# Cross attention and a top-2 expert layer: stack edges filled by engines, biases as a last column of the weights, fewer waits, other orders

## The chip, the core and the metric

The kernel runs on one core of a Trainium2 chip. The metric is the device time of one execution, in microseconds (us). The core has five engines, each with its own instruction queue: TensorE (PE in the rows, its weight loads PEld), VectorE (DVE), ScalarE (ACT), GpSimd (POOL) and SyncE (SP), which here only issues transfers. Transfers of all queues run on 16 DMA engines. On-chip memory is SBUF, 128 partitions; TensorE writes its products to PSUM, of which there are eight banks of 128 x 512 numbers.

## The reference

Four sequences of 256 tokens with 256 features pass through a cross attention with 16 heads of 16 features, then through a layer of 8 experts of which each token uses 2, each with a gated part of 32 units and a low-rank part of 16.

```
x  = x + attention(layernorm(x), ctx)        # Q, K, V each with a bias; softmax(Q K' / 4) V, then @ Wo.T + bo
h  = layernorm(x)
s  = softmax(h @ G); w = s where it is among the two largest, else 0
gated = silu(h @ gate_w) * (h @ up_w)
x  = x + einsum(gated, w, down_w) + einsum(h @ lora_A, w, lora_B)
```

All is in 32-bit floats.

## The kernel before

Each engine has an order written out by hand, a word for each step: `name:b.i@bank` is step `name` of sequence `b` (0 to 3), part `i`, writing to PSUM bank `bank`; `e:0.0-5` is six steps. `plan` (L88) turns a line of `ORDERS` (L46) into a list, and every engine's block walks through its own list. Between engines, `wait` (L198) waits for the counter of a step's name on the engine that does it. A PSUM bank is written again only when the step that empties it is done (`wait_evacuated`, L201). So the orders alone decide what stands behind what.

The attention, for each sequence b:

- st1 and rs1 compute mean and deviation of x, n1 normalises, xT transposes on TensorE and xTE copies the result out of PSUM. q is the product with Wq, k and v the products of the context with Wk and Wv. Products run as plain 32-bit ones (a record each for two halves, so 4 matmuls are 8 records) or, for k and v of sequences 1 to 3 (`KV_PARTS`), as three products of high and low parts in the type fp32r. chi and clo split the context, wkh/wkl and wvh/wvl the weights.
- Scores use *stacks*: `kstack` and `qstack` hold for each head pair 64 rows a head, four rows of each head feature's place: high, high, low part of k, and a last one; rows 3, 7, ... are the *edge*. The edge of `kstack` is -1, that of `qstack` 0, but in row 63 and 127 it later takes the row maximum (ms), which the product then subtracts. khi, kw, klo and qhi, qw, qlo make the parts; ks0 (two transfers), ks1, qs0 (two) and qs1 carry them into the stacks from SBUF to SBUF. There are `NSTACK` = 3 stacks of each kind; sequence 3 uses those of sequence 0 again. For the first, minus and zeros fill the whole stack on VectorE and GpSimd; for the others fillk and fillq (L301 to L315) transfer the edge from a small tile `edge`, and fillq:3 writes zeros over rows 63 and 127 again.
- max computes scores of a head pair for the row maximum, mx (VectorE, L613) reduces them, mrow transposes the maxima, mrE copies them, attn computes the scores again with the maximum subtracted and the other way round, e takes the exponential (ScalarE, L501). u multiplies by v (tiles of 32 columns), uT and un divide by the sum, o is the output product, x2 adds it and x (to which GpSimd's xo has added the output bias).
- The biases: `biases` is a 128 x 6 array with the columns of bq, bk and bv, loaded by biases; obias loads bo for all 128 partitions. bias (L741) multiplies bv by Wo on TensorE, bp (L593) adds it to bo.

The expert layer: mean and mlow compute column means of its weights `wf`, wfc and wlc subtract them, wfh and wfl split them; st2, rs2 are the second normalisation, x2T the transpose, low the product with the low-rank part and the gate, glu the product with gate_w and up_w, th and h the activation, r1, ex, r2, r3 the weights of the experts, wl and wh the weighting, hT and lT transposes, down the last product, res the last sum, out the store.

TensorE's array has three shapes here: all 128 x 128; for max and attn two tiles of 64 rows that run side by side; for u, and for the 16-column mrow, tiles of 32 columns.

Of the kernel before, what the change touches and what calls it, by code (L numbers as in the profile page):

```python
# [5 lines left out]
F32 = mybir.dt.float32  # L6
# [41 lines left out]
        k:0@0 xT:0@1 bias@2 q:0@1 mean@0 k:1@2 xT:1@3 v:1@4 max:0.0@0 max:0.1@6 q:1@3 max:0.2@4 max:0.3@0 xT:2@2  # L48
        k:2@6 max:0.4@4 max:0.5@2 q:2@7 max:0.6@0 max:0.7@4 v:0@6 max:1.0@0 xT:3@2 max:1.1@4 max:1.2@6 mrow:0@3
        q:3@2 max:1.3@0 max:1.4@4 v:2@3 attn:0.0@6 max:1.5@0 attn:0.1@2 max:1.6@4 attn:0.2@6 max:2.0@0 attn:0.3@2  # L50
        attn:0.4@4 max:1.7@6 max:2.1@0 attn:0.5@2 max:2.2@4 mrow:1@6 u:0.0@7 attn:0.6@0 max:2.3@2 u:0.1@7
        max:2.4@4 attn:0.7@0 k:3@6 max:2.5@2 attn:1.0@4 max:2.6@0 u:0.2@7 attn:1.1@2 attn:1.2@4 u:0.3@7 max:2.7@0
        attn:1.3@2 u:1.0@6 attn:1.4@4 mlow@7 attn:1.5@2 u:1.1@6 mrow:2@0 max:3.0@4 attn:1.6@2 max:3.1@0 o:0@6
        max:3.2@4 attn:2.0@2 max:3.3@0 x2T:0@6 u:1.2@7 attn:1.7@2 max:3.4@0 low:0@6 max:3.5@4 max:3.6@2 u:1.3@7
        attn:2.1@0 glu:0.1@6 attn:2.2@4 max:3.7@0 attn:2.3@2 glu:0.0@7 attn:2.4@4 mrow:3@0 attn:2.5@2 u:2.0@1
        u:2.1@1 attn:2.6@4 attn:2.7@2 o:1@0 u:2.2@1 attn:3.0@4 u:2.3@1 x2T:1@0 attn:3.1@2 attn:3.2@4 v:3@7
        low:1@0 attn:3.3@4 attn:3.4@6 glu:1.0@1 attn:3.5@4 o:2@0 attn:3.6@2 u:3.0@6 u:3.1@6 attn:3.7@4 x2T:2@0
# [12 lines left out]
        uT:0.0 mx:2.5-6 un:0.0 uT:0.1 mx:2.7 un:0.1 uT:1.0 mx:3.0-1 x2:0 wlc mx:3.3 mx:3.2 mx:3.4-6 uT:1.1 mx:3.7  # L70
        un:1.1 un:1.0 st2:0 uT:2.0 un:2.0 x2:1 h:0.0-1 r1:0 uT:2.1 st2:1 un:2.1 r2:0 r3:0 x2:2 r1:1 h:1.0 uT:3.0
        st2:2 un:3.0 r2:1 uT:3.1 un:3.1 h:1.1 r3:1 res:0 r1:2 x2:3 st2:3 r2:2 h:2.0 r3:2 r1:3 h:2.1 r2:3 res:1
        r3:3 wl:3 h:3.1 h:3.0 wh:3 res:2 res:3
# [818 lines left out]
```

## Time and profile before

| | us |
|---|---|
| median of 3 runs | 125.38 (125.12 to 125.75) |
| the profiled execution | 126.23 |
| its span, first to last instruction | 124.4 |
| TensorE busy | 112.7 (91%) |
| VectorE busy | 91.1 (73%) |
| ScalarE busy | 66.9 (54%) |
| GpSimd busy | 47.3 (38%) |

The profile is of one execution, the times are of others. A matmul's end is modelled, so a busy TensorE need not be at its peak. In the chain of waits each piece is what the next one waited for, or the work before it on the same engine. A time in a timeline is counted from the first instruction; `[2.43 <-PE ...]` behind a row is idle time of that engine in front of it, and what ended it.

### The profile page before, as it was taken

The numbers are of one execution on the slowest core, as the hardware profiler recorded it, in microseconds if no ns is written. First come the engines' busy times: TensorE is split into PE (matmuls) and PEld (weight loads), VectorE is DVE, ScalarE is ACT, GpSimd is POOL, SyncE is SP. The second block draws the span as 40 slices with busy tenths as digits, with TensorE's granted clock in tenths as the row PEclk, the third lists the DMA queues.
The fourth block names the chain that finished last, engine by engine and source line by source line (L and its number), as shares of the span: only waits on it lengthen the run. The fifth ranks groups of instructions, "written<-read, shape, count | busy, mean of one in ns | idle before, by whom it ended". The sixth has DMA issues, their size and how long they took to land.

```text
span 124.4 us, 2498 instructions
## 1 busy us (share of the span) xinstructions
PE 112.7 (91%) x884; PEld 83.4 (67%) x884; DVE 91.1 (73%) x191; ACT 66.9 (54%) x113; POOL 47.3 (38%) x78
## 2 busy tenths in 40 slices
PE   6970699999999879999999999999999999999790
PEld 6840476978778655856667666578666788866570
DVE  5553274298999999799899797799288688796601
ACT  0570302777866895598655387788957204314300
POOL 7881873076996950040004003025603444240000
PEclk9999558999999999999999999999999999999999
DMA  3979992994294000183000000000000002002022
GB/s 85 344 205 389 386 368 96 310 305 178 84 365 146 3 8 5 65 312 142 5 0 5 0 0 11 0 0 0 5 0 0 0 5 84 0 3 84 0 84 84
DMA packets 9845, 12.96 MB, mean 104 GB/s; under 512 B 922, under 2 KB 6378, under 8 KB 9834
## 3 DMA queue, kind: packets, MB, share of 16 engines
q1 hardware_dynamic: 8458, 11.23, 25.8%
q10 hardware_dynamic: 1376, 1.58, 3.7%
q8 instruction: 7, 0.11, 0.3%
q14 instruction: 4, 0.03, 0.1%
HBM read 4.34 MB, written 1.05 MB: 43 GB/s over the span
## 4 chain that ended last, share of the span: by engine, by line
PE 81%; DMA 8%; ACT 5%; SPq 2%; issue 1%; DVE 1%
PE unit L689 29%; PE unit L798 13%; DMA wo<-woT 8%; PE unit L788 7%; PE unit L772 7%; PE unit L807 6%; ACT probs L501 4%; PE unit L853 3%; PE unit L855 3%; PE unit L854 3%; PE unit L814 2%; PE unit L745 2%; PE unit L752 2%; PE unit L840 1%; PE unit L733 1%; PE unit L778 1%
## 5 line engine op out<-in xcount | busy, mean ns | idle before, releaser
L613 DVE TENSOR_REDUCE rowmax<-unit 128x4 f32<-128x1024 f32 x32 | 37.6, 1220 | 6.0 <-PE unit L772 6.0
L501 ACT ACTIVATE probs<-unit 128x1024 f32<-128x1024 f32 x32 | 31.6, 1030 | 10.3 <-PE unit L788 10.1
L798 PE MATMUL unit<-probs,vaug 128*32 128x256 f32 x256 | 16.5, 384 | 0.0
L788 PE MATMUL unit<-qstack,kstack 64*128 64x256 f32 x128 | 14.3, 310 | 0.5 <-ACT probs L501 0.2
L772 PE MATMUL unit<-kstack,qstack 64*128 64x256 f32 x128 | 13.5, 305 | 0.6 <-DVE rowmax L613 0.3
L788 PEld LDWEIGHTS unit<-qstack,kstack 64*128 64x128 f32 x128 | 9.5, 185 | 6.7 <-issue 4.6
L772 PEld LDWEIGHTS unit<-kstack,qstack 64*128 64x128 f32 x128 | 9.3, 185 | 4.4 <-issue 2.6
L798 PEld LDWEIGHTS unit<-probs,vaug 128*32 128x32 f32 x256 | 7.0, 109 | 5.6 <-issue 1.1
L554 DVE BATCH_NORM_STATS2 stats<-xs 128x6 f32<-128x256 f32 x16 | 5.9, 409 | 6.3 <-DMA xs<-x 6.3
L438 POOL TENSOR_TENSOR x2T_lo<-x2T,x2T_hi 128x512 fp32r<-128x512 f32 x3 | 3.8, 1283 | 16.9 <-ACT x2T L516 16.9
L412 POOL TENSOR_TENSOR k_lo<-k_whole,k_hi 128x512 fp32r<-128x512 f32 x3 | 3.8, 1278 | 15.1 <-ACT k_whole L482 15.1
L689 PE MATMUL unit<-xT,wq 128*128 128x256 f32 x32 | 9.5, 450 | 0.0
L689 PE MATMUL unit<-wf,x2T 128*128 128x136 f32 (+1 forms) x40 | 8.3, 347 | 0.0
L689 PEld LDWEIGHTS unit<-xT,wq 128*128 128x128 f32 x32 | 7.0, 226 | 1.5
L807 PE MATMUL unit<-wo,attnT 128*128 128x256 f32 x32 | 7.9, 389 | 0.0
L617 DVE STREAM_TRANSPOSE uT<-unit 128x512 f32<-128x512 f32 x8 | 5.7, 708 | 2.3 <-PE unit L798 2.3
L482 ACT ACTIVATE q_hi<-unit,bias_sb 128x256 fp32r<-128x256 f32 x8 | 3.4, 471 | 6.7 <-PE unit L689 6.7
L430 POOL TENSOR_SCALAR vare<-mv 128x2 f32<-128x2 f32 x4 | 0.9, 234 | 14.9 <-DVE mv L557 14.9
L745 PE MATMUL unit<-wo,bias_sb 128*128 128x256 f32 x4 | 2.1, 674 | 4.9 <-DMA wo<-woT 4.9
L807 PEld LDWEIGHTS unit<-wo,attnT 128*128 128x128 f32 x32 | 5.8, 190 | 1.1
L689 PEld LDWEIGHTS unit<-wf,x2T 128*128 128x128 f32 x40 | 5.4, 190 | 1.6 <-issue 1.4
L679 DVE TENSOR_TENSOR xs<-unit,xs 128x512 f32<-128x512 f32 x4 | 2.8, 688 | 4.0 <-PE unit L855 4.0
(123 smaller groups left out, 224.7 us busy)
## 6 DMA issues: line engine op xcount, KB each, us to landing
kstack<-k_hi SPq DMA_DIRECT2D x8, 256.0 KB, 3.9
qstack<-q_hi SPq DMA_DIRECT2D x8, 256.0 KB, 2.4
xs<-x SPq DMA_DIRECT2D x4, 256.0 KB, 9.5
kstack<-k_lo SPq DMA_DIRECT2D x4, 256.0 KB, 3.1
qstack<-q_lo SPq DMA_DIRECT2D x4, 256.0 KB, 2.5
out<-xs SPq DMA_DIRECT2D x4, 256.0 KB, 2.1
wf<-wffn ACTq DMA_DIRECT2D x1, 648.0 KB, 11.2
cT<-ctxT ACTq DMA_DIRECT2D x2, 256.0 KB, 6.4
```

The costliest lines, as they stand in the source:

```text
L412: pool.tensor_tensor(lo[:, b % 2], whole[:], hi[:, b % 2].bitcast(F32), ALU.subtract).then_inc(done[name], 1)
L438: pool.tensor_tensor(x2T_lo[:], x2T[:, b % 2], x2T_hi[:].bitcast(F32), ALU.subtract).then_inc(done["x2lo"], 1)
L501: act.activation(probs[:, n % NPAIR], unit[BANK["attn", b, i] // 2][:], ACT.Exp, scale=SCALE)\
L554: ins = dve.bn_stats(stats[:, w, b, t], src[:, t])
L613: dve.tensor_reduce(rowmax[:, b % 2, :, :, i].rearrange("p t j -> p j t"), unit[BANK["max", b, i] // 2][:], AX.X, ALU.max).then_inc(done[" ...
L617: dve.transpose(uT[:, i].rearrange("p h n c -> p (h n c)"), work[BANK["u", b, 2 * i]].rearrange("p h s -> p (h s)")).then_inc(done["uT"], 1)
L689: ins = pe.matmul(dst, left(i, k), right(j, k), start=(n == 0), stop=(n == len(steps) - 1))
L745: ins = pe.matmul(dst[:, 0], bv_sb[:, k:k + 1].to_broadcast([P, P]), wo[:, k], start=(k == 0), stop=(k == KT - 1))
L772: ins = pe.matmul(pair[:, j, t], qstack[b][rows, i, t * P:(t + 1) * P], kstack[b][rows, i], start=True, stop=True)
L788: ins = pe.matmul(pair[:, j, t], kstack[b][rows, i, t * P:(t + 1) * P], qstack[b][rows, i], start=True, stop=True)
L798: ins = pe.matmul(dst[QUAD * j:QUAD * (j + 1), i % 2], vaug[:, b % NVALUE, t, 4 * i + j], probs[:, n % NPAIR, j % 2, t], start=(t == 0), s ...
L807: ins = pe.matmul(dst[:, t], attnT[:, b % 2, k, t * P:(t + 1) * P], wo[:, k], start=(k == 0), stop=(k == KT - 1))
```

## The change

1. *Edges.* The steps minus, zeros, fillk and fillq go. In their place kfill and qfill fill a whole stack, for b below 3: kfill:2 and kfill:0 on VectorE, qfill:0 and qfill:2 on GpSimd, qfill:1 and kfill:1 on ScalarE, as a copy of a column of `edge`, which shrinks to 128 x 2. Every transfer into a stack waits for its fill. Row 63 and 127 are left out of the max product, which so has 63 rows for each tile, and need no zeros.
2. *Biases.* bk, bq and bv become a 257th column of Wk, Wq and Wo, so rows of 1028 bytes are loaded; bo is loaded as one row, and bias adds it with a third product, of one row of ones and that row. bp only copies.
3. *Waits.* `wait` notes for each pair of engines the furthest step waited for, and leaves out a wait for an earlier one.
4. *Orders.* All five are written anew.

```diff
     "scalar": """
-        c:0 wq biases obias c:1 wf wkh wvh khi:0 xTE:0 n1:1 qhi:0 khi:1 xTE:1 kw:1 vE:1 n1:2 qhi:1 qw:1 xTE:2
...
+        c:0 wq c:1 bo qfill:1 kfill:1 wkh wvh khi:0 xTE:0 vE:0 n1:1 qhi:0 xTE:1 n1:2 khi:1 kw:1 qhi:1 qw:1 n1:3
...
+        known = {}
+
         def wait(engine, name, b=0, i=0):
-            engine.wait_ge(raised[ON[name, b, i]][name], TURN[name, b, i])
+            stage = name, b, i
+            if known.get((engine, ON[stage]), -1) < PLACE[stage]:
+                known[engine, ON[stage]] = PLACE[stage]
+                engine.wait_ge(raised[ON[stage]][name], TURN[stage])
+
+        def wait_in(engine, loaded, count=16):
+            if (engine, loaded.name) not in known:
+                known[engine, loaded.name] = count
+                engine.wait_ge(loaded, count)
...
             if name == "wk":
-                engine.dma_start(wk[:], view[:, :, 0:D]).then_inc(wk_in, 16)
+                engine.dma_start(wk[:], view[:, :, 0:D + 1]).then_inc(wk_in, 16)
...
-            if name == "biases":
-                engine.dma_start(bias_sb[:], biases).then_inc(bias_in, 16)
-            if name == "obias":
-                engine.dma_start(bo_sb[:], bo.partition_broadcast(P)).then_inc(out_bias_in, 16)
+            if name == "bo":
+                engine.dma_start(bo_row[:], bo).then_inc(bo_in, 16)
...
-                if name == "fillk":
-                    wait(sp, "edge")
-                    sp.dma_start(kstack[b][3:P:4].bitcast(F32),
-                                 edge[:, 0].bitcast(F32).unsqueeze(1).to_broadcast([QUAD, PAIRS, T])).then_inc(k_stacked[b], 16)
...
                 if name == "ks1":
-                    if b == 0:
-                        wait(sp, "minus")
+                    if b < NSTACK:
+                        wait(sp, "kfill", b)
...
+                if name in ("kfill", "qfill"):
+                    act.wait_ge(raised["vector"]["edge"], 1)
+                    dst, n = (kstack[b], 0) if name == "kfill" else (qstack[b], 1)
+                    act.copy(dst[:].rearrange("p i t -> p (i t)"), edge[:, n:n + 1].to_broadcast([P, PAIRS * T]))\
+                        .then_inc(done[name], 1)
...
                     for o in range(KT):
-                        ins = act.activation(dst[:, o], work[BANK[of, b, 0]][:, o], ACT.Identity, bias=bias[:, o:o + 1])
+                        ins = act.activation(dst[:, o], work[BANK[of, b, 0]][:, o], ACT.Identity, bias=bias[:, o, D:])
...
+                if name == "kfill":
+                    dve.memset(kstack[b][:].bitcast(F32), -1.0).then_inc(done["kfill"], 1)
...
                     for k in range(KT):
-                        ins = pe.matmul(dst[:, 0], bv_sb[:, k:k + 1].to_broadcast([P, P]), wo[:, k],
-                                        start=(k == 0), stop=(k == KT - 1))
-                    ins.then_inc(done["bias"], 1)
+                        pe.matmul(dst[:, 0], wo[:, k, D:].to_broadcast([P, P]), wo[:, k, 0:D], start=(k == 0), stop=False)
+                    pe.matmul(dst[:, 0], warm[0:1], bo_row[:], start=False, stop=True).then_inc(done["bias"], 1)
...
                         for j in range(2):
-                            rows = slice(HALF * j, HALF * (j + 1))
+                            rows = slice(HALF * j, HALF * (j + 1) - 1)
```

The issue queue of SyncE from its start, before. `wk`, `wv`, `wo` and `cT` are weights and context, `xs` is x; names in brackets are what a row waits for.

```order
L252 DMA xs<-x 128x2x256
L257 DMA wk<-wattn 128x2x256
L261 DMA wv<-wattn 128x2x256
L252 DMA xs<-x 128x2x256
L308 DMA qstack<-edge 32x8x256 [waits edge_by_vector]
L269 DMA wo<-woT 128x512
L252 DMA xs<-x 128x2x256
L308 DMA qstack<-edge 32x8x256 [waits edge_by_vector]
L252 DMA xs<-x 128x2x256
L254 DMA cT<-ctxT 128x2x256
L303 DMA kstack<-edge 32x8x256 [waits edge_by_vector]
L323 DMA kstack<-k_hi 32x4x512 [waits khi_by_scalar,minus_by_vector]
```

The same queue in the changed kernel:

```order
L264 DMA xs<-x 128x2x256
L269 DMA wk<-wattn 128x2x257
L273 DMA wv<-wattn 128x2x256
L264 DMA xs<-x 128x2x256 x2
L277 DMA wf<-wffn 128x2x648
L266 DMA cT<-ctxT 128x2x256
L279 DMA wo<-woT 128x514
L325 DMA kstack<-k_lo 32x4x512 [waits kfill_by_vector]
L264 DMA xs<-x 128x2x256
L318 DMA kstack<-k_hi 32x4x512 [waits khi_by_scalar]
```

`wf` has come over from ScalarE's queue; the last load of x (x:2) stands behind the transfer of k_lo and its wait for kfill:0, which stands behind klo:0 on VectorE.

ScalarE from its start, before:

```order
L254 DMA cT<-ctxT 128x2x256
L259 DMA wq<-wattn 128x2x256
L263 DMA bias_sb<-biases 128x6
L265 DMA bo_sb<-bo 128x256
L254 DMA cT<-ctxT 128x2x256
L267 DMA wf<-wffn 128x2x648
L453 ACT_TABLE_LOAD
L453 CAST wk_hi<-wk 128x512 [waits wk_in]
L453 CAST wv_hi<-wv 128x512 [waits wv_in]
L482 ACTIVATE k_hi<-unit,bias_sb 128x256 [waits bias_in,k_by_tensor]
```

and in the changed kernel:

```order
L266 DMA cT<-ctxT 128x2x256
L271 DMA wq<-wattn 128x2x257
L266 DMA cT<-ctxT 128x2x256
L275 DMA bo_row<-bo 1x256
L450 ACT_TABLE_LOAD
L450 CAST qstack<-edge 128x2048 [waits edge_by_vector]
L450 CAST kstack<-edge 128x2048 [waits edge_by_vector]
L455 CAST wk_hi<-wk 128x512 [waits wk_in]
L455 CAST wv_hi<-wv 128x512 [waits wv_in]
L483 ACTIVATE k_hi<-unit,wk 128x256 [waits wk_in,k_by_tensor]
```

Two issues are gone, and two fills of whole stacks stand between the table load and the first cast.

TensorE at its start, before (`warm` is a run without use, `unit` is PSUM; the rows are k:0, xT:0, bias, q:0, mean):

```order
L694 MATMUL unit<-warm 128x128 x10
L689 MATMUL unit<-cT,wk 128x256 x4
L733 MATMUL unit<-ident,xn 128x128 x4
L745 MATMUL unit<-wo,bias_sb 128x256 x2
L689 MATMUL unit<-xT,wq 128x256 x4
L752 MATMUL unit<-wf,mean 128x512 x2
```

and in the changed kernel:

```order
L697 MATMUL unit<-warm 128x128 x10
L692 MATMUL unit<-cT,wk 128x256 x4
L736 MATMUL unit<-ident,xn 128x128 x4
L692 MATMUL unit<-wv,cT 128x256 x4
L692 MATMUL unit<-xT,wq 128x256 x4
L761 MATMUL unit<-wf,mean 128x136 x2
L754 MATMUL unit<-wf,mean 128x512 x2
L748 MATMUL unit<-wo 128x256 x2
L749 MATMUL unit<-bo_row,warm 128x256
```

The product that needs `wo` has moved from in front of q:0 to behind mean, and v:0 and mlow have come forward.

TensorE behind the last row maximum, before: attn:2.4, mrow:3, attn:2.5, u:2.0 and 2.1, attn:2.6 and 2.7, o:1, u:2.2, attn:3.0, u:2.3, x2T:1.

```order
L788 MATMUL unit<-qstack,kstack 128x256 x4
L778 MATMUL unit<-ident,rowmax 16x128 x2
L788 MATMUL unit<-qstack,kstack 128x256 x4
L798 MATMUL unit<-probs,vaug 32x256 x16
L788 MATMUL unit<-qstack,kstack 128x256 x8
L807 MATMUL unit<-wo,attnT 128x256 x4
L798 MATMUL unit<-probs,vaug 32x256 x8
L788 MATMUL unit<-qstack,kstack 128x256 x4
L798 MATMUL unit<-probs,vaug 32x256 x8
L814 MATMUL unit<-ident,xs 128x128 x4
```

and in the changed kernel, from mrow:3 on:

```order
L780 MATMUL unit<-ident,rowmax 16x128 x2
L790 MATMUL unit<-qstack,kstack 128x256 x12
L800 MATMUL unit<-probs,vaug 32x256 x24
L790 MATMUL unit<-qstack,kstack 128x256 x4
L809 MATMUL unit<-wo,attnT 128x256 x4
L790 MATMUL unit<-qstack,kstack 128x256 x12
L800 MATMUL unit<-probs,vaug 32x256 x8
```

Steps of one shape have been put together: three attn steps in a row, three `u` steps in a row. From the last row maximum to the last `u` of sequence 3 the shape changes 23 times before and 15 times now.

## Rows read from the trace of the kernel before

**Rows 1.** The page: the span in 40 slices of 3.11 us, tenths busy.

```profile
PE   6970699999999879999999999999999999999790
...
PEclk9999558999999999999999999999999999999999
DMA  3979992994294000183000000000000002002022
GB/s 85 344 205 389 386 368 96 310 305 178 84 365 146 3 8 5 65 312 142 5 0 5 0 0 11 0 0 0 5 0 0 0 5 84 0 3 84 0 84 84
```

**Rows 2.** The chain of waits: start us, us, what; head, and one later piece.

```profile
3.58 10.06 DMA wo<-woT
...
13.68 2.07 PE unit L745 x4
15.76 3.41 PE unit L689 x8
19.17 1.93 PE unit L752 x4
...
41.50 4.60 ACT probs L501 x5
```

**Rows 3.** Windows: length, busy us (instructions) by engine, clock, DMA share, GB/s.

```profile
24.30:72.90 48.60, 47.55 (x454) 34.36 (x454) 43.91 (x46) 35.00 (x57) 19.89 (x22) 1.00 0.30 107
72.90:121.20 48.30, 47.32 (x357) 34.50 (x355) 35.26 (x118) 24.27 (x43) 13.10 (x26) 1.00 0.05 18
```

**Rows 4.** The chain of waits: pieces behind another shape and behind their own.

```profile
30.31 1.92 PE unit L689 x8
...
48.72 1.00 PE unit L798 x16
49.72 0.43 PE unit L772 x4
50.16 0.24 PE unit L788 x4
...
57.69 0.66 PE unit L759 x4
...
74.65 1.86 PE unit L798 x32
...
100.91 1.73 PE unit L807 x8
```

**Rows 5.** Timeline of VectorE: start us, us, line, operation, idle time before it.

```profile
27.44 2.36 DVE L613 TENSOR_REDUCE rowmax<-unit 128x4 f32<-128x1024 f32 x2 [0.23 <-PE unit L772]
```

**Rows 6.** Timeline of all engines: instructions of the head, and a longer cast.

```profile
1.96 1.76 DVE L567 MEMSET kstack<- 128x2048 f32 x1 [0.38 <-issue]
...
3.85 1.28 ACT L453 ACT_TABLE_LOAD   x1 [3.85 <-issue]
...
4.22 0.48 SPq L252 DMA_DIRECT2D xs<-x  x1
...
5.82 0.62 ACT L453 CAST wk_hi<-wk 128x512 fp32r<-128x512 f32 x1 [0.68 <-DMA wk<-wattn]
...
8.77 0.59 ACT L469 COPY xT<-unit 128x512 f32<-128x512 f32 x1
...
14.93 0.75 DVE L554 BATCH_NORM_STATS2 stats<-xs 128x6 f32<-128x256 f32 x2 [3.19 <-DMA xs<-x]
...
21.14 1.29 DVE L600 TENSOR_TENSOR wf<-wf,unit 128x512 f32<-128x512 f32 x2 [0.18 <-PE unit L752]
24.85 2.36 DVE L613 TENSOR_REDUCE rowmax<-unit 128x4 f32<-128x1024 f32 x2 [2.43 <-PE unit L772]
...
36.37 1.05 ACT L456 CAST wf_hi<-wf 128x1024 fp32r<-128x1024 f32 x1
```

**Rows 7.** DMA issues: line, engine, count, KB each, median us from issue to landing.

```profile
kstack<-k_lo SPq DMA_DIRECT2D x4, 256.0 KB, 3.1
qstack<-q_lo SPq DMA_DIRECT2D x4, 256.0 KB, 2.5
```

More of the change, by code:

```diff
@@ L47 @@
     "tensor": """
[L48 to L57, printed above, removed]
@@ L58 @@
-        hT:0@1 lT:0@6 glu:1.1@7 u:3.2@1 u:3.3@1 low:2@0 down:0@6 o:3@7 glu:2.0@6 lT:1@0 hT:1@1 x2T:3@7 glu:2.1@0
-        low:3@1 down:1@2 lT:2@3 glu:3.1@4 hT:2@5 glu:3.0@0 lT:3@1 down:2@2 hT:3@0 down:3@0
+        k:0@0 xT:0@1 v:0@2 q:0@1 mlow@0 mean@2 bias@3 xT:1@4 k:1@5 max:0.0@0 max:0.1@6 q:1@3 max:0.2@0 max:0.3@4
+        max:0.4@6 v:1@2 max:0.5@0 xT:2@3 k:2@6 max:0.6@0 max:0.7@2 q:2@7 max:1.0@4 max:1.1@0 mrow:0@6 k:3@2
+        max:1.2@4 max:1.3@6 v:2@3 max:1.4@0 attn:0.0@4 max:1.5@6 attn:0.1@2 attn:0.2@4 max:1.6@0 max:2.0@2 xT:3@6
@@ L67 @@
+        wfh xTE:2 vE:1 khi:2 kw:2 qhi:2 mrE:0 qw:2 khi:3 kw:3 vE:2 e:0.0-2 xTE:3 e:0.3-4 e:0.6 mrE:1 e:0.5 qhi:3
+        e:0.7 qw:3 e:1.0-3 vE:3 e:1.4-5 mrE:2 e:1.6 x2hi:0 e:1.7 x2w:0 e:2.0 lowE:0 e:2.1-4 mrE:3 th:0.1 e:2.5
+        ex:0 e:2.6-7 e:3.0-3 th:0.0 e:3.4-6 x2hi:1 lTE:0 x2w:1 e:3.7 lowE:1 hTE:0 th:1.0 ex:1 x2hi:2 x2w:2 th:1.1
+        lowE:2 ex:2 x2w:3 lTE:1 th:2.1 th:2.0 lowE:3 hTE:1 th:3.1 ex:3 hTE:2 lTE:2 th:3.0 lTE:3 hTE:3
     """,
     "vector": """
-        warm edge minus st1:0 n1:0 st1:1 st1:2 klo:0 bp st1:3 qlo:0 wfc mx:0.0-7 mx:1.0-6 mx:2.0 mx:1.7 mx:2.1-4
@@ L70 @@
[L70 to L73, printed above, removed]
+        warm edge kfill:2 st1:0 n1:0 st1:1 klo:0 kfill:0 wlc qlo:0 st1:2 st1:3 bp wfc mx:0.0-2 mx:0.4-5 mx:0.3
@@ L77 @@
-        xo:1 xo:3 qlo:2 clo:3 xo:2 qlo:3 wfl xo:0 klo:3 x2lo:0 rs2:0 x2lo:1 rs2:1 wl:0 wh:0 rs2:2 x2lo:2 wl:1
-        wh:1 rs2:3 wl:2 wh:2
+        ident earlier qfill:0 ones rs1:0 wkl rs1:1 wvl chi:1 clo:1 rs1:2 rs1:3 chi:2 clo:2 qlo:1 klo:1 chi:3
+        clo:3 qfill:2 klo:2 qlo:2 xo:3 xo:0 klo:3 xo:1 xo:2 wfl qlo:3 x2lo:0 rs2:0 wl:0 wh:0 x2lo:1 rs2:1 rs2:2
+        x2lo:2 wl:1 rs2:3 wh:1 wl:2 wh:2
     """,
     "sync": """
-        x:0 wk wv x:1 fillq:2 wo x:2 fillq:1 x:3 c:2 fillk:1 ks0:0 wd ks1:0 qs0:0 qs1:0 c:3 fillk:2 ks0:1 ks1:1
@@ L82 @@
-        qs0:1 qs1:1 qs0:2 ks1:2 ks0:2 ms:0 qs1:2 ms:1 fillq:3 qs0:3 qs1:3 ks0:3 ks1:3 ms:2 ms:3 out:0 out:1 out:2
-        out:3
+        x:0 wk wv x:1 x:3 wf c:3 wo ks1:0 x:2 ks0:0 qs0:0 qs1:0 c:2 wd ks0:1 qs0:1 qs1:1 ks1:1 ks0:2 ms:0 qs0:2
+        ks1:2 qs1:2 ms:1 ks1:3 qs0:3 ks0:3 qs1:3 ms:2 ms:3 out:0 out:1 out:2 out:3
     """,
@@ L583, in _ @@
                     of = name[0]
-                    hi, lo, bias = (k_hi, k_lo, bk_sb) if of == "k" else (q_hi, q_lo, bq_sb)
+                    hi, lo, bias = (k_hi, k_lo, wk) if of == "k" else (q_hi, q_lo, wq)
                     if b >= 2:
@@ L593, in _ @@
                 if name == "bp":
[L594 to L596 removed]
+                    dve.wait_ge(raised["tensor"]["bias"], 1)
+                    dve.tensor_copy(bo_sb[:], work[BANK["bias", 0, 0]][:, 0]).then_inc(done["bp"], 1)
                 if name == "wfc":
[L598 removed]
+                    dve.wait_ge(raised["tensor"]["mean"], 1)
                     for k in range(KT):
@@ L603, in _ @@
                 if name == "wlc":
-                    wait(dve, "mlow")
+                    dve.wait_ge(raised["tensor"]["mlow"], 1)
                     for k in range(KT):
@@ L762, in _ @@
                     if i == 0:
-                        if b == 0:
-                            wait(pe, "minus")
-                            wait(pe, "zeros")
+                        if b < NSTACK:
+                            wait(pe, "kfill", b)
+                            wait(pe, "qfill", b)
                         wait_stacked(pe, "k", b)
```

134 lines of the change are left out of this document (65 added, 69 removed).

## The prediction, made before the changed kernel had run

> **What bounds the kernel now.** Read the slices first [rows 1]: from slice 7 on TensorE is busy nine or ten tenths almost to the end, at full clock. The first 21 us are another matter: an idle stretch in slices 3 and 4, and half the clock (1.2 of 2.4 GHz) in slices 4 and 5, after that idleness. The chain of waits [rows 2] says what the head is: 10.06 us for the transfer of `wo`, for which bias waits in front of q:0; then bias, q:0 and mean, 2.07, 3.41 and 1.93. A product of q's size at full clock takes 1.73 [rows 4], so q:0 alone lost 1.7 us to the clock. From the first maximum at 24.4 to 121.1 the chain is nearly all TensorE; the one other large piece is 4.60 us of exponentials, where the two kinds of score step alternate [rows 2].
>
> Next, who else is near the bound. I cut the rest where the last row maximum ends [rows 3]. From 24.3 to 72.9 TensorE is busy 47.55 us and VectorE 43.91 of 48.6; the maxima come in pairs of 2.36 with gaps of 0.23 [rows 5]. Both are full, and a gain of one alone is worth little. From 72.9 to 121.2 TensorE is busy 47.3 of 48.3 and VectorE 35.3: there TensorE alone sets the time.
>
> **What a change of tile shape costs** [rows 4]. A score step (four matmuls on 64-row tiles) takes 0.43 behind another shape, 0.24 behind its own: 0.19. A full-array product of 8 records takes 1.92 behind scores and 1.73 behind its own shape: 0.19. Two `u` steps take 1.86, one takes 1.00: 0.14. I take 0.19 on average. The row transposes mrow use 16 columns and count with `u`.
>
> **The head, step by step.** Gone are biases, obias and four 256 KB fills from `edge`, with a 16 KB one; `wf` moves to SyncE's queue ahead of `wo`, and x:2 moves behind the first stack transfer.
> - *Transfers.* Of what is gone, fillq:2, biases and obias share the queues with `wo` and `wf` now. Slice 2 shows the DMA engines 90% busy or more at 205 GB/s, against 389 and 386 in slices 4 and 5 [rows 1]; the 24-byte rows of biases and the broadcast of `bo` are what is peculiar to it. In the change, `wf` and all that may go with it (x:0, wk, wv, x:1, x:3; c:0, wq, c:1) are 2.8 MB. 85 and 344 GB/s over two slices of 3.11 us are 1.3 MB by 6.2 us; the rest at 385 takes 3.8, and with about one for the end of a transfer `wf` lands near 11, `wo` near 12.3, against 14.5 and 13.6 now.
> - *ScalarE.* Four issues instead of six end at 2.8, then the table load of 1.28 [rows 6]. The fills qfill:1 and kfill:1 have no row. Casts of 512 and 1024 columns take 0.62 and 1.05, so 2048 should take 1.05 + 2 x 0.43 = 1.91 each; below that stands VectorE's fill of the same tile, 1.76, above it four casts of 512, 2.48 [rows 6]. I take the casts' slope, the same kind of instruction. So 4.1 + 3.8 = 7.9; wkh and wvh to 9.2, khi:0 (0.84, two activations) to 10.0, xTE:0 (0.59 [rows 6]) to 10.6, vE:0 and n1:1 (0.6 and 1.1) to 12.3, qhi:0 to 13.2. The fills lie on the path of q:0: without them it could start 1.8 us earlier.
> - *TensorE.* xT:0 ends at 8.7 as now; v:0, pulled forward, fills until 10.5 (1.72), so there is no pause and I expect the full clock. q:0 from 10.6 to 12.3; mlow 0.46 (its piece of 0.66 less a change [rows 4]); mean 1.72; bias 0.86, and its third product, of one row of `bo`, 0.43 and two changes: 16.2. xT:1 0.44 and k:1 1.4: 18.0. No row shows a product with one row; between 0.43 and 1.1, it isn't last here.
> - *Stacks and the first maximum.* VectorE: klo:0 to 10.9, kfill:0 (1.76) to 12.7. Only then does SyncE issue ks1:0, and x:2, ks0:0, qs0:0, qs1:0 are queued behind that wait. Issues take 0.55 to 0.6 each, so qs1:0 goes out at 16.2 and lands 2.5 later, 18.7 [rows 7]. x:2, issued at 13.4, has no row on an idle queue. By q_lo's 2.5 and k_lo's 3.1 [rows 7] it lands near 16.4; by its own time now, issued 4.22 and read 14.93 [rows 6], it takes 10.7 and lands at 24. I take 3.0, as only `wo` and c:3 are ahead of it and nearly done. VectorE then does st1:2 and st1:3 (1.0 each), bp (0.4) and wfc (1.29 [rows 6]): **first maximum at 20.1**, against 24.85 now [rows 6], a gain of **4.75**. Bounds: 19.2 if x:2 isn't last (the stacks are), 23 if TensorE falls to the low clock.
>
> By the Trainium skill, DMA: Bandwidth & Descriptors, How a descriptor splits into AXI transactions, a row that does not begin on a 256-byte boundary costs beats for bytes that are thrown away; this speaks against the extra column, which makes rows of 1028 bytes at an odd pitch. Estimated from that page, the four loads concerned would take about a fifth longer, some 0.5 us in the head; no row here shows such a load.
>
> **From the first to the last maximum.** TensorE has 42 changes of shape in this stretch, before and after. glu:0.1, mlow and v:0 leave it (1.39 + 0.46 + 1.72), two attn steps, v:1 and v:3 enter (0.47 + 2.83): 0.27 less. VectorE has wlc out (0.5) and st2:0 in (1.0). Both engines are full, so 48 us stay 48: **0**. The bounds: -2.7, if the waits under the 4.60 us of exponentials go, to +2.1, two exponentials more for ScalarE that nothing hides.
>
> **Behind the last maximum.** 15 changes of shape instead of 23: 8 x 0.19 = 1.5. glu:0.1 comes in, v:3 and two attn steps are out: 1.42 + 0.47 - 1.39 = 0.5. TensorE sets the time alone here, so **2.0** arrives, unless ScalarE gets in front: from the last maximum to the last attn TensorE has 14.6 us of steps, and ScalarE 11 exponentials of 1.03 with some 3 us beside them.
>
> **Edits with one answer.** The built program keeps the 64-row tile for maxima of 63 rows, so their price stays. Of the waits left out I make nothing: the steps of 0.24 carry waits now and show no gap. A bias read from the weights' last column changes no instruction's size. fillq:3, 16 KB, was hidden.
>
> **Sum.** The profiled execution took 126.23, with a span of 124.4; it lies 0.85 above the median of 125.38. 4.75 + 0 + 2.0 = 6.75 makes it 119.5, and the median **118.6**.
>
> **Rivals.**
> *The middle gains too.* From 40.9 to 46.2 eleven score steps of 0.24, 2.6 us, take 5.3. The new order mixes xT:3 and other steps in. If that returns 2.0, and x:2 isn't last (0.7), the time is 115.9. For it: the gaps of [rows 5] end with TensorE. Against it: VectorE has 44 us to do in those 48.
> *The low clock stays.* If `wf` lands at 14 or later, TensorE idles behind q:0 as it does now behind xT:0; mean and bias, xT:1 and k:1 then run at [rows 2]'s prices, 3 us more: 121.6. Against it: the transfers left out ahead of `wf`.
> *The second half waits.* If the 8 changes are no saving, or ScalarE is late by as much, 2.0 stays away: 120.6. For it: a long row of full-array work now stands at the end, with little between the exponentials.
> *Slower.* Everything on VectorE up to the first maximum, and n1:2 with khi:1 behind it on ScalarE, is now queued behind x:2, which is issued behind the waits for klo:0 and kfill:0. If x:2 takes its present 10.7 instead of 3.0, the first maximum is at 27.8, TensorE stands idle for 8 us and comes back at the low clock, 1 us at least: 118.6 + 7.7 + 1.0 = 127.3. It decides from a landing 9 us after the issue. Against it: at 13.4 hardly a load is ahead.
>
> **Chances.** Forecast (117 to 120) 0.50; middle gains 0.17; low clock 0.12; second half waits 0.15; slower 0.04; in all, a time within 0.5% of now 0.02 (about what a measurement of this kernel can tell from no change). The range of 8 in 10 takes in the rivals on the fast side: 115.6 to 121.6. Faster 0.94, same 0.02, slower 0.04.
>
> **What would show it.** Right: no wait for `wo` in the chain; a granted clock of 1.00 from 6 to 21; two instructions near 1.9 on ScalarE at 4 to 8; first rowmax near 20; the last one ends 47 to 49 later; 46 from there to the last product. Wrong: q:0 later than 11.5, a clock under 1 behind 9, more than 49 between first and last maximum, or TensorE waiting over 1 us in all for ScalarE behind it.

## The result, and the profile after

The changed kernel takes 120.03 us (median of 4 runs, 119.24 to 121.01), the kernel before 125.32 in the same rounds: a ratio of 0.960, with a 95% interval of 0.9545 to 0.9656. The profiled execution took 120.67, with a span of 118.9. The four took 120.67, 119.24, 119.38 and 121.01 us, at mean clocks of 1.0, 1.0, 1.0 and 0.986. A ratio here and below leaves out the executions that are more than 1.5% above the fastest of their kernel, while medians and ranges are those of all.

The page of the changed kernel, the slices that answer to [rows 1], of 2.97 us each (all slices are counted from 0):

```profile
PE   6989997799998799989999999999999999999780
...
PEclk9999999999999999999999999999999999999999
DMA  2998079845627000580000000000000000202022
GB/s 77 361 367 301 0 269 342 284 176 218 258 81 281 8 0 1 206 313 23 0 11 0 0 1 10 0 0 0 6 0 0 0 0 0 88 8 88 0 88 88
```

The idle stretch and the half clock of slices 3 to 5 are gone, and slice 2 moves 367 GB/s where it moved 205. What is left of the head's idleness is in slices 6 and 7.

The chain of waits of the changed kernel, its head, which answers to [rows 2] (start us, us, what):

```profile
1.28 4.95 DMA wk<-wattn
...
6.27 3.79 PE unit L692 x8
...
10.09 0.85 ACT k_hi L483 x2
...
12.21 1.78 DVE kstack L568
14.01 0.65 SPq L325
...
17.87 3.58 DMA qstack<-q_lo
```

No piece waits for `wo` any more. In its place stands the filling of the first stack: k:0 (L692), khi:0, klo:0, the fill kfill:0 on VectorE (L568), then six issues of SyncE in a row, and behind them qs1:0 with its landing of 3.58. The timeline of the changed kernel shows the rows of this stretch, against [rows 6]:

```profile
4.26 1.90 ACT L450 CAST qstack<-edge 128x2048 fp32r<-128x2048 f32 x1
...
6.06 1.89 ACT L450 CAST kstack<-edge 128x2048 fp32r<-128x2048 f32 x1
...
17.27 0.69 PE L749 MATMUL unit<-bo_row,warm 1*128 1x256 f32 x2
...
17.70 0.75 DVE L555 BATCH_NORM_STATS2 stats<-xs 128x6 f32<-128x256 f32 x2 [1.62 <-DMA xs<-x]
...
21.59 0.74 PE L774 MATMUL unit<-kstack,qstack 63*128 63x256 f32 x8 [1.64 <-DMA qstack<-q_lo]
...
22.14 2.36 DVE L616 TENSOR_REDUCE rowmax<-unit 128x4 f32<-128x1024 f32 x2 [0.99 <-PE unit L774]
```

Windows of the changed kernel, columns as in [rows 3], cut where the last maximum ends:

```profile
22.10:69.10 47.00, 45.60 (x460) 33.80 (x457) 43.91 (x48) 35.45 (x58) 23.38 (x24) 1.00 0.29 109
69.10:115.70 46.60, 45.61 (x346) 33.88 (x344) 34.97 (x114) 22.76 (x41) 12.38 (x23) 1.00 0.06 18
```

So the profiled executions differ in three places: first maximum at 22.14 instead of 24.85, 2.71 us; from it to the end of the last one 46.99 instead of 48.06, 1.07; from there to the last product 46.48 instead of 48.20, 1.72. Together 5.50 of the 5.56 between 126.23 and 120.67.

### The profile page after: what moved, and what is told of

It reads as the page before. It is cut to its first block, busy times and chain, and to the rows that moved or that the text cites. A ratio compares the mean times of both kernels' runs of the same rounds, so it can differ in the third digit from the quotient of the medians.

```text
span 118.9 us, 2315 instructions
## 1 busy us (share of the span) xinstructions
PE 110.0 (93%) x886; PEld 83.1 (70%) x886; DVE 91.5 (77%) x192; ACT 70.4 (59%) x115; POOL 49.4 (42%) x79
## 4 chain that ended last, share of the span: by engine, by line
PE 62%; DVE 12%; DMA 10%; SPq 5%; issue 3%; ACT 2%; POOL 1%; POOLq 1%; DVEq 0%; ACTq 0%
PE unit L692 19%; PE unit L800 12%; PE unit L790 8%; PE unit L774 7%; DMA qstack<-q_lo 6%; PE unit L809 5%; DMA wk<-wattn 4%; PE unit L855 2%; PE unit L857 2%; PE unit L856 2%; DVE rowmax L616 2%; SPq L333 2%; DVE kstack L568 1%; PE unit L816 1%; SPq L325 1%
## 5 line engine op out<-in xcount | busy, mean ns | idle before, releaser
L774 PE MATMUL unit<-kstack,qstack 63*128 63x256 f32 x128 | 12.7, 302 | 2.3 <-DMA qstack<-q_lo 2.3
L790 PE MATMUL unit<-qstack,kstack 64*128 64x256 f32 x128 | 13.2, 304 | 0.8 <-ACT probs L502 0.5
L774 PEld LDWEIGHTS unit<-kstack,qstack 63*128 63x128 f32 x128 | 9.1, 186 | 5.7 <-issue 4.0
L289 POOL TENSOR_TENSOR low<-low,weight_low 128x128 f32<-128x128 f32 x6 | 2.3, 403 | 14.5 <-DVE weight_hid L668 14.5
L692 PE MATMUL unit<-wf,x2T 128*128 128x136 f32 (+1 forms) x40 | 8.2, 344 | 0.0
L692 PE MATMUL unit<-xT,wq 128*128 128x256 f32 x32 | 7.8, 386 | 0.0
L409 POOL TENSOR_TENSOR q_lo<-q_whole,q_hi 128x512 fp32r<-128x512 f32 x3 | 3.9, 1284 | 7.5 <-ACT q_whole L483 7.5
L532 ACT ACTIVATE hid<-unit,half_rstd 128x256 f32<-128x256 f32 x8 | 3.8, 474 | 5.1 <-PE unit L692 5.1
L692 PEld LDWEIGHTS unit<-wf,x2T 128*128 128x128 f32 x40 | 5.7, 190 | 1.3 <-issue 1.0
L692 PEld LDWEIGHTS unit<-xT,wq 128*128 128x128 f32 x32 | 5.8, 190 | 0.9
L697 PE MATMUL unit<-warm 128*128 128x128 f32 x20 | 4.6, 430 | 1.1 <-DVE warm L566 1.1
```

Of the source, the lines that this page charges most:

```text
L409: pool.tensor_tensor(lo[:, b % 2], whole[:], hi[:, b % 2].bitcast(F32), ALU.subtract).then_inc(done[name], 1)
L692: ins = pe.matmul(dst, left(i, k), right(j, k), start=(n == 0), stop=(n == len(steps) - 1))
L697: pe.matmul(unit[3][:, 1, 0, 0:P], warm[:], warm[:], start=True, stop=True)
L774: ins = pe.matmul(pair[:, j, t], qstack[b][rows, i, t * P:(t + 1) * P], kstack[b][rows, i], start=True, stop=True)
L790: ins = pe.matmul(pair[:, j, t], kstack[b][rows, i, t * P:(t + 1) * P], qstack[b][rows, i], start=True, stop=True)
```

## The experiments

Three groups of kernels ran, each with the kernel before beside it, which took 125.68 us (e1 to e4), 125.70 (e5 to e8) and 125.26 (e9 to e12) in the median; so 0.4 us between two groups says little. Each experiment is told by three marks of its profiled execution: start of the first maximum, length from there to the end of the last, length from there to the last product. The kernel before has 24.85, 48.06 and 48.20, the changed one 22.14, 46.99 and 46.48.

### Orders alone: is it the place of bias?

In the kernel before, bias goes behind mean, and bp behind wfc:

```diff
-        k:0@0 xT:0@1 bias@2 q:0@1 mean@0 k:1@2 xT:1@3 v:1@4 ...
+        k:0@0 xT:0@1 q:0@1 mean@0 bias@2 k:1@2 xT:1@3 v:1@4 ...
```

> The kernel before with one step moved: TensorE does bias behind mean instead of in front of q:0 (and VectorE does bp behind wfc). All transfers, fills, waits and the rest of the orders stay. Theory A (the head was lost because bias waits for wo in front of q:0, an order, not the transfers): q:0 starts near 9.5 us instead of 15.8 and costs 1.9 instead of 3.4; then wf, which landed at 14.5, is last, mean and bias follow it, and the first row maximum comes 2 to 3 us earlier: 122.5 to 123.5. Theory B (what counts is the transfers that the fills and biases put in front of wo and wf): mean still waits for wf, the clock still falls in that wait, and the time stays within 1 us of 125.3.

Measured: 127.34 us (126.52 to 127.9), ratio 1.0121 (1.0077 to 1.0166): 1.2% slower, with the first maximum at 25.96 instead of 24.85. Neither theory had that. Its timeline:

```profile
9.85 1.97 PE L689 MATMUL unit<-xT,wq 128*128 128x256 f32 x8 [1.06 <-ACT xT L469]
...
16.32 3.78 PE L752 MATMUL unit<-wf,mean 128*128 128x512 f32 x4 [4.51 <-DVE k_lo L589]
```

q:0 runs as soon as xT:0 is there, 5.7 us earlier. But mean then waits 4.5 us. It writes the PSUM bank of k:0, which klo:0 has to empty first, and on VectorE klo:0 stood behind st1:2 and the landing of x:2 (read at 14.47). Mean itself runs at half speed, 3.78 for [rows 2]'s 1.93. The wait moved on to the next late transfer, so the place of bias alone was not the head's cost. That the late transfers were is what the next run shows.

### The change with the old orders

Edges, biases and waits as in the change, the five orders as before, as far as they can be.

> The changed kernel's code (fills by engines, bias columns, fewer waits, 63-row maxima) with the orders of the kernel before; the removed steps are taken out and the fills put in at near places (kfill:0 and kfill:2 early on VectorE, qfill:0 and qfill:2 on GpSimd, qfill:1 and kfill:1 behind the loads on ScalarE). Theory A (the orders carry the gain: bias moved, steps of one shape put together): only the shorter head of transfers is left. wo lands near 10 instead of 13.6, so 2 to 3 us come back in the head and nothing behind it: 122.5 to 123.5. Theory B (code and transfers carry it): 120 to 121. The end behind the last row maximum should stay at 48 us by A.

Measured: 120.97 us (120.36 to 121.67), ratio 0.9606 (0.9544 to 0.9667), the same as the change. Marks: 19.51, 47.93, 48.00. Windows and the head's wait:

```profile
19.51:67.44 47.93, 47.01 (x449) 33.65 (x446) 43.91 (x46) 34.40 (x56) 21.40 (x23) 1.00 0.27 101
67.44:115.44 48.00, 47.30 (x357) 34.49 (x355) 35.61 (x116) 24.24 (x43) 13.09 (x26) 1.00 0.05 18
```

```profile
10.35 1.13 PE L749 MATMUL unit<-wo 128*128 128x256 f32 x4 [1.60 <-DMA wo<-woT]
```

This splits the change. Edges, biases and waits bring 5.34 us of head and little elsewhere (48.06 to 47.93, 48.20 to 48.00), though bias still stands in front of q:0: `wo` lands 7.5 us after its issue instead of 10.06. The new orders bring 0.94 in the middle and 1.52 behind, and lose 2.63 in the head. About 1 us of that loss belongs to the profiled execution of the change alone, in which k:0 ran slowly: where it ran fast, the first maximum is at 20.98 (e3) and 21.11 (e10), a loss of 1.5 to 1.6. In the medians the orders bring nothing. At a mean clock of 1.0 they may bring 1 us: 120.36 and 120.50 here, 119.24, 119.38 and 120.67 in the change.

### All waits made

```diff
-            if known.get((engine, ON[stage]), -1) < PLACE[stage]:
+            if True:
...
-            if (engine, loaded.name) not in known:
+            if True:
```

> The changed kernel with every wait made again, also those for steps that an earlier wait already covers; nothing else changes. My prediction put the left-out waits at zero: 119.2 to 120.8, as the changed kernel. The rival: TensorE pays for a wait that is already met. It has about 100 of them more; at 20 ns each behind the first maximum that would be 1.5 to 2 us: 121.5 to 122.

Measured: 120.7 us (119.81 to 121.55), ratio 0.9559 (0.9479 to 0.9639). Its two runs at a mean clock of 1.0 took 119.81 and 119.94, those of the change 119.24, 119.38 and 120.67, so in the times the waits stay inside the spread. The trace shows more. From the end of the last maximum to the last product e3 takes 46.8 us, and the change and the seven other kernels that have its orders in this stretch (e4, e6, e7, e8, e10, e11, e12) all take 46.5. Up to the end of glu:1.0, 21.0 us behind the last maximum, e3 and the change are alike, so TensorE's own row pays nothing there. The loss comes later, where the work goes through VectorE and GpSimd, and part of it is a wait of TensorE for GpSimd that the change does not have; first the change, then e3:

```profile
103.78 0.65 PE L842 MATMUL unit<-ident,hid 128*128 128x128 f32 x4
```

```profile
104.58 0.63 PE L842 MATMUL unit<-ident,hid 128*128 128x128 f32 x4 [0.26 <-POOL hid L298]
```

So leaving waits out brings 0.3 us behind the last maximum, by one trace of e3 against eight, and perhaps 0.5 in all.

### The fill of the first stack taken off the path

```diff
-        warm edge kfill:2 st1:0 n1:0 st1:1 klo:0 kfill:0 wlc qlo:0 ...
+        warm edge kfill:0 st1:0 n1:0 kfill:2 st1:1 klo:0 wlc qlo:0 ...
```

First together with twelve warm-up products instead of ten (e4), then the fill alone (e7), then the warm-up alone (e10).

> The changed kernel with two changes in the head: kfill:0 goes to the front of VectorE (kfill:2 takes its place behind n1:0), so that ks1:0 waits for klo:0 only and SyncE's row behind it starts 2.0 us earlier; and 12 useless products instead of 10 in front of k:0, which close the pause of 0.5 us before it, after which k:0 ran at half speed (3.78 instead of 1.99). Theory A (both lie on the path to the first row maximum: k:0 - khi:0 - klo:0 - kfill:0 - ks1:0 ... qs1:0): first maximum at 18.5 to 19.5 instead of 22.1, time 117 to 118, and the runs lie closer together than 119.2 to 121.0. Theory B (the landing of the stacks or x:2 takes up what the fill gives): first maximum at 21 or later, 119 to 120.

> The changed kernel with kfill:0 at the front of VectorE alone, with the 10 useless products. It parts the run that had both edits. If the fill carries the gain, first maximum near 20 and 118 to 118.5 in the runs in which k:0 runs at full speed, and 1.8 us more in those in which it doesn't; if the pause in front of k:0 carries it, 119 to 120.

> The changed kernel with twelve warm-up products instead of ten, and nothing else. It asks whether the idle time in front of k:0 is what makes k:0 run at half speed (3.8 us instead of 2.0) in some runs. Theory A (the pause matters): k:0 near 2.0 in every run, runs close together at 119.2 to 119.5. Theory B (the pause does not matter): runs spread from 119.2 to 121, median near 120.0 as for the changed kernel.

Measured: e4 117.75 us (117.58 to 117.83), ratio 0.9347 (0.9308 to 0.9385), marks 19.28, 46.90, 46.49; e7 117.79 (117.74 to 117.84), ratio 0.9384 (0.933 to 0.944), marks 19.25, 46.94, 46.48; e10 120.95 (119.44 to 122.05), ratio 0.962 (0.9551 to 0.969), first maximum 21.11. The fill alone brings all of it: 2.2 us in the median. The warm-up brings nothing, and its theory A fell: k:0 took 2.12 us in the profiled execution, and the time was 120.95 all the same. Nor does the pause in front of k:0 decide its speed. In the change k:0 waited 0.54 us and took 3.79. In e3, whose head is the same, it waited 0.74 and took 1.99, and in e5, told below, it waited longer still:

```profile
5.92 1.99 PE L693 MATMUL unit<-cT,wk 128*128 128x256 f32 x8 [0.98 <-DMA wk<-wattn]
```

What made it slow in the change stays open.

The chain of e10 is the forecast's own path, and shows each of its steps at its size:

```profile
4.28 1.90 ACT qstack L450
6.17 1.32 ACT kstack L450
...
9.78 0.88 DVE k_lo L593 x2
10.66 0.38 issue
11.03 1.77 DVE kstack L568
...
16.67 3.57 DMA qstack<-q_lo
```

Two rows of e10's timeline show what follows the wait, then one of e7's, with the fill off the path:

```profile
20.37 1.13 PE L774 MATMUL unit<-kstack,qstack 63*128 63x256 f32 x8 [2.31 <-DMA qstack<-q_lo]
...
21.43 3.20 PE L692 MATMUL unit<-xT,wq 128*128 128x256 f32 x8
```

```profile
18.71 0.74 PE L774 MATMUL unit<-kstack,qstack 63*128 63x256 f32 x8 [0.74 <-DMA qstack<-q_lo]
```

After 2.3 us of idleness the score step and q:1 ran slowly, at a granted clock of 0.72 from 18 to 24 us. e10's four runs took 119.44, 120.95, 120.96 and 122.05 us at mean clocks of 1.0, 0.986, 0.986 and 0.966; where TensorE waits 0.74 us (e7), four runs lie within 0.1 us. So the fill on the path costs twice: its own time, and in some runs the clock. In the traces of e10 and e7 that is 1.86 us up to the first maximum, and another 1.35 from there to the end of the last (48.29 against 46.94).

### The fills as transfers again

The kernel with the old orders (e2), with the edges of stacks 1 and 2 carried by four transfers of 256 KB as before, and no fill on ScalarE; the biases stay a column.

> As the run with the old orders, but the edges of stacks 1 and 2 are filled by transfers again (fillk and fillq, 4 x 256 KB, at their old places), and the two casts on ScalarE and the fills kfill:2 and qfill:2 are gone; the biases stay columns of the weights. It parts the changed code into its two halves. Theory A (the fills in front of wo and wf were most of the head: fillq:2 is 256 KB ahead of wo, and biases only 3 KB): wo lands at 12 to 13, first maximum at 22.5 to 23.5, time 123.5 to 124.5. Theory B (the loads of biases with their 24-byte rows were it): wo lands near 10.5 and ScalarE is 3.8 us free, first maximum at 19 to 20, 120 to 121 as with the fills on engines.

Measured: 125.11 us in the median of ten runs between 122.27 and 126.55, at mean clocks from 0.998 down to 0.954; the ratio, 0.9809 (0.9747 to 0.9871), rests on the three fastest. The profiled execution, 126.43, is one of the longest, so its marks (25.39, 47.94, 48.04) overstate the head. Its timeline:

```profile
11.74 2.07 PE L749 MATMUL unit<-wo 128*128 128x256 f32 x4 [1.69 <-DMA wo<-woT]
...
14.89 3.78 PE L693 MATMUL unit<-xT,wq 128*128 128x256 f32 x8
```

The half clock is back, as in the kernel before. Since the time goes with the clock, compare runs of one clock. At 0.983 to 0.986 the kernel before takes 124.3 to 125.2 us, e5 123.2 and 123.3, e2 121.4 and 121.7. So the four transfers cost some 1.7 us net of the work that the engines' fills put in their place, and what e5 shares with the change (biases, `bo`, waits) brings 1 to 2. The rest of what the transfers cost is the clock: seven of e5's ten runs were at 0.972 or lower, none of e2's four. With the clock, e5 stands 4.1 us above e2 in the median, and the kernel before 4.7. The landings show the transfers at work. The first two transfers of k_hi land 6.7, 7.0 and 7.3 us after their issue in the kernel before, e1 and e5, and 3.0 to 3.2 in the change and e2.

### Single transfers, each by itself

A load of 128 rows of 24 bytes, as biases was, added to e4 at its old place, into a tile that nothing reads (e6); the broadcast of `bo`, 128 KB, added to the kernel e8 of the next heading at its old place (e11); four transfers of the kind of fillk and fillq, 1 MB, added to e8 (e12).

> The fastest kernel so far (fill 0 first, 12 useless products) with one transfer more: 128 rows of 24 bytes into an unused tile, behind wq in ScalarE's queue, where biases was loaded before; nothing uses it, the last engine only waits for it at the end. It prices the small rows alone. Theory A (small rows take engine time out of all proportion): a slice near 200 GB/s comes back, wf lands 1.2 to 1.6 us later than at 7.3 after its issue, TensorE waits for it behind q:0, and the time rises by 0.5 to 1.5 to 118.3 to 119.3. Theory B (128 packets are nothing; the broadcast and the fills were the slow part): wf lands within 0.4 us, 117.8.

> The kernel of e8 with one more load, of 128 KB: bo for all 128 partitions, issued by ScalarE where before issued it, into a tile that nothing reads. Theory A (it shares the queues with what is loaded at the time and slows it by its share): wf and wo land 0.3 to 0.4 us later than in e8, the time stays within 0.3 of 116.84. Theory B (the broadcast is what held slice 2 of the kernel before at 205 GB/s): wf lands 1 us later or more, and mean behind it, 117.3 or more.

> The kernel of e8 with four more transfers of 256 KB each on SyncE's queue, of the kind of fillk and fillq (32 rows of 1 KB, each repeated eight times), behind x:1, x:3, c:3 and the third of them. They write into the tile of the exponentials before it is used; the stacks are filled by the engines as in e8. Theory A (these transfers were the cost of the head of the kernel before): 1 MB at some 380 GB/s puts wf back by 1.4 us and wo and x:2 by 2.8, the clock falls in some runs, 118.5 to 121. Theory B (the queues have room while ScalarE fills): within 0.5 of 116.84.

Measured: e6 117.7 us (117.68 to 117.82), nothing against e4's 117.75, and `wf` lands 7.4 us after its issue instead of 7.3: theory B. e11 117.98 (117.91 to 118.25), ratio 0.9428 (0.9394 to 0.9461), against e8's 116.84: 1.1 us. e12 119.62 (119.5 to 119.69), ratio 0.9553 (0.9527 to 0.958): 2.8 us. The rate in the slices of e11's page:

```profile
GB/s 62 359 222 389 385 367 255 161 278 140 147 277 92 6 0 45 371 139 0 6 6 0 0 11 0 0 0 0 6 0 0 0 0 0 90 8 90 0 90 90
```

The broadcast makes slice 2 fall from e8's 354 to 222 GB/s, near the 205 of [rows 1]. In e5, which has the fills' transfers but not the broadcast, slice 2 is at 373. So the slow slice is the doing of one 128 KB load. `wf` lands 8.8 us after its issue instead of 7.4, `wo` 9.1 instead of 7.7, as theory B said. But mean did not wait for `wf`, so the 1.1 us did not come the way I had written. The chain of e11 shows it:

```profile
3.63 1.28 ACT L453
...
12.45 3.88 DMA xs<-x
16.35 0.76 DVE stats L558 x2
```

ScalarE starts its table load at 3.63 instead of 2.95, since it issues one load more and the one for `bo` takes 0.77 instead of 0.57, and this puts x:2's issue back from 11.77 to 12.45. Then x:2 is read 3.88 after its issue instead of 3.20, and is now last in the head: first maximum at 19.73 instead of 18.37, half from each. In e12 the price is on SyncE's queue:

```profile
4.91 1.45 SPq L278 DMA_DIRECT2D wf<-wffn  x1
6.40 1.66 SPq L267 DMA_DIRECT2D cT<-ctxT  x1
...
9.43 1.51 SPq L280 DMA_DIRECT2D wo<-woT  x1
```

In e8 the issues of `wf`, c:3 and `wo` take 0.52, 0.47 and 0.47. So SyncE is held up: qs1:0 goes out at 16.05 instead of 14.41, and takes 4.1 us to land instead of 3.0. That the issues are slow because the queues are full is argued, not shown. Theory A had the time, but not the clock: it stayed at 0.999 or more in all four runs.

### A better head, and a try at the middle

From the trace of e7: kfill:0 first, kfill:2 behind klo:0, ks0:0 (whose data is ready first) in front of ks1:0, qhi:0 in front of n1:1, and twelve warm-up products (e8).

> The changed kernel with 12 useless products, kfill:0 first, and three steps moved in the head: kfill:2 from in front of st1:1 to behind klo:0 (it held st1:1 for 0.8 us), qhi:0 in front of n1:1 on ScalarE (it waited 0.8 us behind it), ks0:0 in front of ks1:0 on SyncE, so that 1.2 us of its issues lie before klo:0 is done. If the path to the first maximum is now qhi:0, qlo:0, qs1:0 and its landing of 3.5 us: qs1:0 is issued at 14.2 to 14.5 instead of 15.1, the first maximum is at 18.4 to 18.8 instead of 19.3, and the time 117.0 to 117.3. If k:1, which ends at 18.0, is what is late, only 0.2 us are left to win: 117.6.

Measured: 116.84 us (116.81 to 117.19), ratio 0.9318 (0.925 to 0.9385), marks 18.37, 46.89, 46.48. This is the best version, 3.2 us under the change. Its first score step runs behind k:1 with no idleness in front of it (`max:0.0` at 17.82), and the stack is no longer waited for:

```profile
17.82 0.74 PE L774 MATMUL unit<-kstack,qstack 63*128 63x256 f32 x8
...
18.37 2.36 DVE L616 TENSOR_REDUCE rowmax<-unit 128x4 f32<-128x1024 f32 x2
```

What holds the head now is ScalarE. The chain of e8 goes through its two fills to khi:0, xTE:0 and q:0, and from there on TensorE works without a gap. Moving these fills was not tried:

```profile
4.25 1.90 ACT qstack L450
6.14 1.33 ACT kstack L450
```

Then the same for stack 2 in the middle (e9): qw:2, qfill:2 and ks1:2 earlier.

> The kernel of e8 with stack 2 filled and transferred sooner: qw:2 in front of mrE:0 on ScalarE, qfill:2 four steps earlier on GpSimd, ks1:2 in front of qs0:2 on SyncE. In e8 TensorE waits 0.46 us for exponentials and 0.49 us for the transfer of q_lo between 34 and 36 us. Theory A (stack 2 holds up the middle): that wait shrinks, and the time is 116.1 to 116.5, against 116.84 for e8. Theory B (VectorE's maxima and ScalarE's exponentials fill the middle anyway, so the wait only moves): 116.7 to 117.0, the stretch from first to last maximum 46.9 as in e8.

Measured: 118.18 us in the median; the runs took 117.56 and 117.59 at a clock of 1.0, 118.76 at 0.985, and the profiled one 177.02 at 0.573. The first three are slower than e8 by 0.7 and more, which neither theory had. But e8 ran in another group, and the ratios to the kernel before, 0.9423 (0.9365 to 0.948) here and 0.9318 (0.925 to 0.9385) there, overlap. So the edit won nothing, and that it lost is likely but not sure. The trace is of the execution at half the clock, so where the 0.7 went stays open.

## Why the prediction was right, and where it was off

The median came out at 120.03: faster, as forecast, inside the range of 115.6 to 121.6, and 1.4 above the 118.6. Of the 6.75 us of the sum 5.50 arrived. The head fell short by 2.04, and 1.07 in the middle, which I had put at nothing, made up half of it; that the total came so near is in this part luck. By the steps of the sum:

**The head: 4.75 forecast, 2.71 measured.** This is the term that was mis-sized. Most single steps held. The transfers did: `wf` landed at 11.0 (forecast 11) and `wo` at 12.3 (12.3), though the 389 and 386 GB/s that I put in slices 4 and 5 are those of slices 3 and 4, counted as slice 2 is. The fills on ScalarE took 1.90 and 1.89, forecast 1.91. In e10, where k:0 ran fast, khi:0 ended at 9.76 (10.0), klo:0 at 10.66 (10.9) and kfill:0 at 12.80 (12.7); x:2 landed 3.0 us after its issue, as I took it, far from the rival's 10.7. I put x:2 last, with the maximum at 20.1, and the stacks next, at 19.2. It was the stacks, and they came 1.9 us later: qs1:0 was issued at 16.67 instead of 16.2 (0.47), it landed 3.57 later instead of 2.5 (1.07), and the first score step then took 0.37 longer to its maximum. That is 21.11 in e10. The profiled execution of the change had a k:0 of 3.79 us on top, which pushed q:0 back to 12.40, past the 11.5 that I had named as a sign of being wrong, qs1:0 to 17.87 and the maximum to 22.14. The largest failed step is the landing. I took 2.5 from [rows 7], a median over other moments of the kernel before; here five stack transfers and x:2 go out in the 4 us ahead of it. In the change that median is 3.7. That the crowd ahead is the reason is argued, not shown. For it: in e2, with three stack transfers in the 4 us ahead, the first q_lo landed 2.5 us after its issue, and in e8, with four and x:2, 3.0. Against it: in e1 three were ahead, and it took 4.1.

**What I missed besides was a place.** I had counted kfill:0 at 1.76 us between klo:0 and ks1:0, and let it stand as a step like others, since x:2 seemed last. e7 shows what that place costs: 1.9 us of first maximum against e10, and 2.2 us of time against the change.

**The middle: 0 forecast, 1.07 measured.** e2 shows that it is the orders (47.93 against 46.99). I had said that both engines are full. VectorE's busy time is indeed the same to 0.01 us, 43.91, so all that could go was its idleness. Groups of VectorE's maxima (busy, mean ns | idle before them), without the first two; first of the kernel before, then of the change:

```profile
L613 DVE TENSOR_REDUCE rowmax<-unit 128x4 f32<-128x1024 f32 x30 | 35.2, 1220 | 3.6 <-PE unit L772 3.6
```

```profile
L616 DVE TENSOR_REDUCE rowmax<-unit 128x4 f32<-128x1024 f32 x30 | 35.4, 1221 | 2.7 <-PE unit L774 2.6
```

The idle time in front of the maxima fell from 3.6 to 2.7. The many gaps of 0.23 that I had shown in [rows 5] gave little of it. Nearly all, 0.78, is one gap, in front of the last maximum; first the kernel before, then the change:

```profile
71.68 1.23 DVE L613 TENSOR_REDUCE rowmax<-unit 128x4 f32<-128x1024 f32 x1 [0.95 <-PE unit L772]
```

```profile
67.90 1.23 DVE L616 TENSOR_REDUCE rowmax<-unit 128x4 f32<-128x1024 f32 x1 [0.17 <-PE unit L774]
```

e2, with the old orders, still has the 0.95. Before, glu:0.1 stood ahead of the last max product on TensorE, and VectorE waited behind it; in the change glu:0.1 comes behind that product. My sums had this step as TensorE work that leaves the middle and comes in behind; they asked how much work there was, and not where VectorE waited for it. The rival in which the middle gains too had the right direction and half its size: 1.07 for its 2.0. The mechanism that it names, the stretch under the exponentials, was not tested by itself. The bound of a full engine is its busy time, and 4.1 us were left above it.

**Behind the last maximum: 2.0 forecast, 1.72 measured.** The 8 changes of shape hold: pieces of the change's chain, against [rows 4]:

```profile
69.65 0.91 PE unit L790 x12
70.56 2.73 PE unit L800 x48
```

Three score steps in a row take 0.91, one of 0.43 and two of 0.24; three `u` steps take 2.73, one of 1.00 and two of 0.865, so 0.14 is saved by each that follows another. e2 against the change gives 1.52 for the orders, changes and work moved together, for 1.5 and 0.5 forecast; the trace cannot part the two. The other 0.2 is there with the old orders too (48.20 to 48.00), and the waits left out are its likely source (e3). TensorE waited for ScalarE once, 0.8 us in front of L855, as it did before (0.9).

**Edits with one answer.** Waits: I made nothing of them, and the trace of e3 shows 0.3 us behind the last maximum. The product of one row took 0.69, within 0.43 to 1.1. By the Trainium skill, DMA: Bandwidth & Descriptors, How a descriptor splits into AXI transactions, a row that does not begin on a 256-byte boundary costs beats for bytes that are thrown away. The estimate that I had worked out from that page for rows of 1028 bytes was some 0.5 us in the head. The landings, first of the kernel before, then of the change (KB each, us from issue):

```profile
wk<-wattn SPq DMA_DIRECT2D x1, 256.0 KB, 4.5
```

```profile
wk<-wattn SPq DMA_DIRECT2D x1, 257.0 KB, 4.9
```

Over the kernels with 1028-byte rows `wk` takes 4.2 to 4.9, with 1024-byte rows 4.2 (e1) and 4.5. Nothing like 0.5 us shows; a cost of 0.2 would be lost in that spread, since other loads share the queues.

**A guess that held by half.** I named two things as peculiar to the slow slice 2, the 24-byte rows of biases and the broadcast of `bo`. e6 clears the first (349 GB/s in slice 2 with these rows), e11 shows that it is the second.

## What to carry to other kernels

When a transfer leaves the path, list every step between the next late data and its use, and look first for one that needs no data at all: a fill, a table load or a memset on that path belongs in front of it. The gain of a new order can be eaten by one such step (here 2.5 us won in the middle and behind, and 1.5 or more lost in the head), so test new data paths and new orders apart. An engine that is "full" still has its gaps: compare the length of a stretch with its busy time before calling it a bound, and look at each large gap by itself. And when the times of a kernel spread by more than what you look for, as with the waits, compare a stretch of the trace that is the same in every other run.
